# The output bias of a routed expert layer, taken off TensorE: ScalarE multiplies it by the gate, GpSimd adds it to the token rows

## The reference, cut to what matters

```python
logits = n @ Wr + br
probs = softmax(logits)
G, idx = max(probs), argmax(probs)        # gate and expert of the token
h1 = relu(n @ W1[idx] + b1[idx])
out = x + G * (h1 @ W2[idx] + b2[idx])    # b2 is the output bias
```

## Time and profile before

| what | value |
| --- | --- |
| time of 3 runs | median 529.25 us, 528.96 to 532.93 |
| the profiled execution | 533.77 us, of which the span is 532.0 us |
| mean granted TensorE clock | 0.986 of full speed |
| busy in the span | PE 486.3 us, DVE 429.0, ACT 335.7, POOL 81.9 |

### The profile page before, as it was taken

One profiled execution on the slowest core, in us unless ns is written; L12 is line 12 of the kernel. 1 busy time (PEld: TensorE's weight loads), 2 busy tenths in 40 slices (PEclk: granted clock), 3 DMA queues, 4 the chain that ended last, 5 costly groups with the idle time before them and its releaser, 6 DMA issues.

```text
span 532.0 us, 11423 instructions
## 1 busy us (share of the span) xinstructions
PE 486.3 (91%) x4369; PEld 361.9 (68%) x4370; DVE 429.0 (81%) x874; ACT 335.7 (63%) x636; POOL 81.9 (15%) x94
## 2 busy tenths in 40 slices
PE   3999999993899999999998999989899999999994
PEld 3877776761899998997887644444466697776662
DVE  7958889896999999876888778975877787986961
ACT  7356666668799999972775723435444558866820
POOL 5000000000000000001221201213244411222232
PEclk9999999997899999999999899999999999999999
DMA  7970000002011111001000293000011129975111
GB/s 200 311 275 1 1 2 1 2 1 103 2 51 55 56 72 71 2 10 72 2 1 1 99 329 146 1 0 4 1 42 42 62 66 380 338 236 182 55 57 55
DMA packets 25267, 45.10 MB, mean 85 GB/s; under 512 B 6977, under 2 KB 7013, under 8 KB 25212
## 3 DMA queue, kind: packets, MB, share of 16 engines
q1 hardware_dynamic: 23228, 39.16, 21.5%
q0 software_dynamic: 1952, 5.18, 2.6%
q10 hardware_dynamic: 32, 0.01, 0.0%
HBM read 33.23 MB, written 11.95 MB: 85 GB/s over the span
## 4 chain that ended last, share of the span: by engine, by line
PE 36%; DVE 20%; DMA 5%; issue 5%; POOL 4%; ACT 3%; POOLq 0%; DVEq 0%
PE sums L1690 13%; PE sums L1526 7%; PE sums L1703 5%; PE sums L1915 4%; DMA out<-aux 2%; DMA aux<-xperm_scratch 2%; DVE st L901 2%; POOL row L528 2%; PE sums L1886 2%; DVE work L1156 1%; PE sums L1504 1%; DVE big L1319 1%; POOL out L512 1%; PE sums L1680 1%; ACT rings L570 1%
## 5 line engine op out<-in xcount | busy, mean ns | idle before, releaser
L1690 PE MATMUL sums<-big,work 128*128 128x130 f16 x1080 | 66.4, 223 | 8.7 <-DVE work L1156 8.7
L1690 PEld LDWEIGHTS sums<-big,work 128*128 128x128 f16 x1080 | 63.7, 100 | 10.2 <-issue 6.2
L1591 PE MATMUL sums<-big 128*128 128x180 f16 x320 | 60.2, 272 | 1.0 <-DVE big L1005 1.0
L1005 DVE TENSOR_TENSOR big<-mid 128x1024 f16<-128x1024 f16 (+1 forms) x88 | 59.4, 732 | 0.0
L1791 PE MATMUL sums<-mid 128*128 128x512 f16 x200 | 47.2, 379 | 0.0
L1703 PE MATMUL sums<-big,mid 128*128 128x260 f16 x400 | 47.0, 275 | 0.1
L1550 PE MATMUL sums<-big,rings 128*128 128x512 f16 x120 | 45.2, 377 | 0.4
L595 ACT ACTIVATE mid<-sums 128x180 f32 x80 | 26.5, 332 | 28.6 <-PE sums L1598 27.7
L1703 PEld LDWEIGHTS sums<-big,mid 128*128 128x128 f16 x400 | 38.2, 96 | 7.5 <-issue 0.3
L683 ACT ACTIVATE aux<-aux,small 128x1250 f16<-128x1250 f32 x32 | 40.9, 1326 | 2.5 <-DVE work L1156 1.7
L683 ACT ACTIVATE mid<-aux,small 128x1250 f16<-128x1250 f32 x32 | 40.8, 1323 | 2.4 <-DVE work L1156 2.4
(11 more groups left out here) (322 smaller groups left out, 1098.8 us busy)
## 6 DMA issues: line engine op xcount, KB each, us to landing
big<-in_L_ffn_W SPq DMA_DIRECT2D x10, 1024.0 KB, 9.7
mid<-in_L_ffn_W SPq DMA_DIRECT2D x6, 1024.0 KB, 14.1
xperm_scratch<-work SPq DMA_DIRECT2D x1, 5753.0 KB, 18.7
aux<-thr_scratch SPq DMA_DIRECT2D x8, 640.0 KB, 3.8
aux<-xperm_scratch SPq DMA_DIRECT2D x8, 523.0 KB, 3.9
row<-in_x SPq DMA_DIRECT2D x1, 1280.0 KB
aux<-in_L_gnn_Ws SPq DMA_DIRECT2D x4, 256.0 KB, 4.6
row<-in_x SPq DMA_DIRECT2D x1, 1024.0 KB, 7.9
```

Source lines behind the costliest of these rows:

```text
L1005: return V.tensor_tensor(out.rearrange("p c (v two) -> p c v two", two=2), values.rearrange("p (v two) -> p v two", two=2).unsqueeze(1).to ...
L1591: mm(count_bank(base, k)[:, 0:RW], L_ring[:, slot, k * CH + j, :], R_ring[:, slot, k * CH + j, :], start=j == 0, stop=False)
L1690: ins = mm(acc_region(h, t), weighted[i // 2 % NC][:, s % 2, t * P:(t + 1) * P], VP[:, s, part, h, :, :].rearrange("p b f -> p (b f)"), st ...
```

## The change

b2 is no longer split, nor multiplied on TensorE; the 16 products, the selection matrix and the f16 parts go. SyncE loads the row of expert e, copied to all 128 partitions, into one of two buffers (`gb_bc`, `be_bc`), experts 0 and 1 ahead of the tokens, expert e (from 2) after `b2_scaled` has told that e - 2 is used up, and ahead of the load of the tokens of e + 2. VectorE makes the gate in a step of its own, `gate_of(e)`. ScalarE's `scale_bias(e)` multiplies the bias by the gate of each slot into `num_words`, a single buffer for both halves, so each half waits for GpSimd to have added the one before. GpSimd's `add_bias(e)` adds it to the rows in `xs`, once ScalarE has normalised them (`xs_normed`), and VectorE's `result(e)` waits for it (`b2_added`).

```diff
--- before.py
+++ after.py
@@ -211,8 +211,7 @@
         xT16, o = carve(work, 0, [2, 2, K, S1], F16)
         hT16, o = carve(work, o, [2, 2, K, S1], F16)
         h32 = xT_ring[:, :, :, :].rearrange("p a k m -> p (a k m)")[:, 0:4 * S1].rearrange("p (a b m) -> p a b m", a=2, b=2)
-        b2_nat = gb_bc[0:64, :]
-        b2_16 = be_bc[0:64, 0:D // 2].bitcast(F16)
+        b2_bc = [gb_bc, be_bc]
         W0T = [carve(work, 0, [2, D])[0][:, 0, :], carve(work, 0, [2, D])[0][:, 1, :], xh_ring[:, 0, :], xh_ring[:, 1, :]]
         thrT, _ = carve(rings, 0, [NP])
         hs, o = carve(work, 0, [2, D])
@@ -291,7 +290,6 @@
         iotaJ = sb("iotaJ", [P, NO])
         wr_sum = sb("wr_sum", [P, E1])
         valid = sb("valid", [P, 1])
-        pick16 = sb("pick16", [64, E1], F16)
 
         sums = ctx.enter_context(nc.psum_tensor("sums", [P, 8, 512], F32))
         bank = [sums[:, i, :] for i in range(8)]
@@ -402,9 +400,12 @@
             for e in range(3):
                 load_weights(e)
 
-            sp.wait_ge(sem("b2_zeroed"), 1)
-            for q in (0, 32):
-                sp.dma_start(b2_nat[q:q + E1, :], b2_d).then_inc(sem("ld_b2"), 16)
+            def load_bias(e):
+                sp.dma_start(b2_bc[e % 2][:, :], b2_d[e, :].partition_broadcast(P)).then_inc(sem(f"ld_b2_{e % 2}"), 16)
+
+            sp.wait_ge(sem("h_used"), T)
+            load_bias(0)
+            load_bias(1)
 
             sp.wait_ge(sem("scattered"), 16 * T)
             sp.wait_ge(sem("xs_psum"), 2)
@@ -422,6 +423,8 @@
                     sp.wait_ge(sem("w_lo0"), e - 2)
                     sp.wait_ge(sem("w_lo1"), e - 2)
                     load_weights(e + RW32 - 3)
+                sp.wait_ge(sem("b2_scaled"), 2 * (e - 1))
+                load_bias(e)
                 if e + 2 in range(RX, E1):
                     sp.wait_ge(sem(f"put{(e + 2) % RX}"), 32 * ((e + 2) // RX))
                     load_tokens(e + 2)
@@ -502,7 +505,6 @@
 
             g.wait_ge(sem("h_used"), T)
             nc.gpsimd.iota(slots, [[1, S1]], base=0, **kw)
-            nc.gpsimd.memset(b2_nat, 0.0).then_inc(sem("b2_zeroed"), 1)
 
             def put(e):
 
@@ -528,8 +530,21 @@
                     nc.gpsimd.tensor_tensor(x[:, t, :], x[:, t, :], rtmp[:, t % 2, :], ALU.add).then_inc(sem("x4_made"), 1)
                 if t >= 3:
                     scatter(t - 3)
+            def add_bias(e):
+
+                r = e % RX
+                if e:
+                    g.wait_ge(sem("xs_normed"), 2 * e)
+                for j, m in enumerate((P, S1 - P)):
+                    g.wait_ge(sem("b2_scaled"), 2 * e + j + 1)
+                    xr = xs[0:m, r, j, 0:D]
+                    nc.gpsimd.tensor_tensor(xr, xr, num_words[0:m, 0:D], ALU.add).then_inc(sem("b2_added"), 1)
+
+            add_bias(0)
             for e in range(E1):
                 put(e)
+                if e + 1 < E1:
+                    add_bias(e + 1)
             n = g.value_load(nspill[0:1, 0:1], min_val=0, max_val=NO)
             with g.If(n > 0):
                 g.wait_ge(sem("o_pos"), 1)
@@ -766,8 +781,6 @@
             w_hi(0, 0)
             w_hi(0, 1)
             a.wait_ge(sem("ff_used"), T)
-            a.wait_ge(sem("ld_b2"), 32)
-            act(b2_16, b2_nat, ACT.Copy, scale=WS).then_inc(sem("b2_hi"), 1)
 
             def relu(t):
                 a.wait_ge(sem("agg_done"), t + 1)
@@ -820,6 +833,16 @@
                     lg_x = xs[:, r, j, D + 3:ROW]
                     act(lg_x, lg_x, ACT.Exp, accum_out=gsum[:, r, j:j + 1]).then_inc(sem("gates_summed"), 1)
 
+            def scale_bias(e):
+
+                r = e % RX
+                a.wait_ge(sem(f"ld_b2_{e % 2}"), 16 * (e // 2 + 1))
+                a.wait_ge(sem("gate_made"), e + 1)
+                for j, m in enumerate((P, S1 - P)):
+                    if 2 * e + j:
+                        a.wait_ge(sem("b2_added"), 2 * e + j)
+                    act(num_words[0:m, 0:D], b2_bc[e % 2][0:m, :], ACT.Copy, scale=gate[0:m, r, j:j + 1]).then_inc(sem("b2_scaled"), 1)
+
             def x_hi(e):
 
                 if e >= 2:
@@ -850,12 +873,15 @@
             a.wait_ge(sem("ld_xs0"), 16)
             gates(0)
             w_hi(1, 1)
+            scale_bias(0)
             x_hi(2)
             for e in range(E1):
                 if e >= 1 and e + 2 < E1:
                     x_hi(e + 2)
                 if e + 1 < E1:
                     hidden(e + 1)
+                if e:
+                    scale_bias(e)
                 if e == 0:
                     rows(3)
                     w_hi(3, 0)
@@ -1321,9 +1347,6 @@
 
             split_w(0, 0)
             split_w(0, 1)
-            V.tensor_tensor(pick16[:, :], ident16[0:64, 0:E1], ident16[0:64, 32:32 + E1], ALU.add)
-            v.wait_ge(sem("b2_hi"), 1)
-            V.scalar_tensor_tensor(b2_16[32:64, :], b2_nat[32:64, :], WS, b2_16[32:64, :], ALU.mult, ALU.subtract).then_inc(sem("b2_lo"), 1)
 
             def logits(t):
 
@@ -1428,26 +1451,35 @@
                     link(V.tensor_copy(hT16[:, e % 2, 0, f, :], h32[:, q, :, :]))
                     V.tensor_tensor(hT16[:, e % 2, 1, f, :], h32[:, q, :, :], hT16[:, e % 2, 0, f, :], ALU.subtract).then_inc(sem("h_lo16"), 1)
 
+            def gate_of(e):
+
+                r = e % RX
+                v.wait_ge(sem("gates_summed"), 2 * (e + 1))
+                V.reciprocal(gate[:, r, :], gsum[:, r, :]).then_inc(sem("gate_made"), 1)
+                v.wait_ge(sem("gate_made"), e + 1)
+                link(V.tensor_scalar(gate_ws[:, r, :], gate[:, r, :], 1.0 / WS, None, ALU.mult))
+
             def result(e):
 
                 r = e % RX
                 at_least(v, "xs_normed", 2 * e)
                 names(e)
-                v.wait_ge(sem("gates_summed"), 2 * (e + 1))
-                link(V.tensor_scalar(gate[:, r, :], gsum[:, r, :], WS, None, ALU.mult))
-                link(V.reciprocal(gate_ws[:, r, :], gate[:, r, :]))
                 for j, m in enumerate((P, S1 - P)):
                     v.wait_ge(sem("m2_done"), 2 * e + j + 1)
+                    v.wait_ge(sem("b2_added"), 2 * e + j + 1)
                     V.scalar_tensor_tensor(xs[0:m, r, j, 0:D], bank[4 + 2 * (e % 2) + j][0:m, :], gate_ws[0:m, r, j:j + 1],
                                            xs[0:m, r, j, 0:D], ALU.mult, ALU.add).then_inc(sem("res_made"), 1)
 
             h_split(0)
             x_lo(1)
             split_w(2, 0)
+            gate_of(0)
             result(0)
             x_lo(2)
             split_w(1, 1)
             for e in range(E1):
+                if e >= 1:
+                    gate_of(e)
                 if e >= 1 and e + 2 < E1:
                     x_lo(e + 2)
                 if e + 1 < E1:
@@ -1908,16 +1940,14 @@
                     pe.wait_ge(sem("res_made"), 2 * (e - 1))
                 for j in blocks:
                     m = (P, S1 - P)[j]
-                    mm(bank[4 + 2 * (e % 2) + j][0:m, :], pick16[:, e:e + 1].to_broadcast([64, m]), b2_16, start=True, stop=False)
                     for n, (k, (wp, hp_)) in enumerate((k, c) for k in range(K) for c in PARTS):
                         if n % (K // 2 * len(PARTS)) == 0:
                             pe.wait_ge(sem("h_lo16"), 2 * e + k // 2 + 1)
                         ins = mm(bank[4 + 2 * (e % 2) + j][0:m, :], hT16[:, e % 2, hp_, k, j * P:j * P + m],
-                                 W16[e % 2][1][:, wp, k, :], start=False, stop=n == 3 * K - 1)
+                                 W16[e % 2][1][:, wp, k, :], start=n == 0, stop=n == 3 * K - 1)
                     ins.then_inc(sem("m2_done"), 1)
 
             m1_first()
-            pe.wait_ge(sem("b2_lo"), 1)
             m2(0, (0,))
             pe.wait_ge(sem("te_ready"), 1)
             token_T(1)
```

## The result

The changed kernel took 542.16 us (median of 4 runs, 539.2 to 542.69), the kernel before 529.76 us beside it (4 runs, 528.96 to 532.93). The ratio is 1.0199, with a 95% interval of 1.0149 to 1.0249: the change makes it slower. By the ratio that is 10.5 us (7.9 to 13.2); the two medians lie 12.4 us apart. The forecast was 539 us, in a range of 532 to 545.

A forecast was written before the change was run, and what follows sets the result against it. TensorE was taken to bound the kernel, VectorE close behind. Layouts gave +10.4 or +9.1, taken as +10.0, less 0.5 before the loop: +9.5 on 533.77 us makes 543.3, or 539 us on the median, range 532 to 545.

The forecast's parts named there:

- Bias products: TensorE in the expert loop: removing 16 bias products wins 5.3 us, a turn becoming 10.4 us if nobody needs more.
- Prices: New steps in the loop: ScalarE scale 0.75 us, GpSimd add 1.10 us (upper end 2.07), hand-over some 0.05 us.
- Before the loop: First tile's statistics no longer wait for VectorE's selection matrix and low part: -0.5 us taken, between 0 and -0.7.
- The first result: Scale and add steps ahead of the loop's first result start m1(2) 2.6 us late; m1(3), m1(4) recover to +1.9, +1.7.
- The circle of 10.7 us a turn: Loop: gate, scale, add, scale, w_hi, split, token numbers and result, split sum to 10.7 us, already as long as TensorE's 10.4.
- Tokens without reserve: Loop: late put of expert 2 delays token load and everything behind rows(6); m1(6) starts at 504.5 instead of 497.7, +6.8 us.
- TensorE waiting for x_lo in three turns or more: Sign expected in the changed kernel's loop profile: TensorE waits for VectorE's x_lo in at least three turns.
- The end: From expert 6's second result to the kernel's end, expert 7's adds standing behind put(6): 9.8 us, where it was 9.1.
- The sum: Whole kernel: +10.0 us from the layouts, -0.5 before the loop, so +9.5 on 533.77, giving 543.3 us.
- Without that exclusion the layout ends 6 us earlier: Loop and end: if GpSimd adds and VectorE's two-input instructions did not block each other, the laid-out kernel ends 6 us earlier.
- no exclusion: Rival: adds touch VectorE in few places, so only first result, circle and end count: +3.4 to +5.1, 533 us; chance 0.14.
- long-adds rival: Rival: adds meet splits each turn (1.5 us mean) or TensorE's clock falls in new waits: +13 to +16, 544 us; chance 0.16.

The follow-up runs named there:

- e1: The changed kernel with the bias left out altogether (no scale, no add, no waits for them; gate step stays): 528.44 us, ratio 0.993 to the kernel before.
- e11: The kernel before, bias products kept, with selection matrix and f16 bias parts made just ahead of the expert loop: 531.81 us, ratio 0.9968.
- e12: The changed kernel with only the next expert's gate made earlier, right behind the hidden split: 540.93 us, ratio 1.0159 to the kernel before.
- e5: The changed kernel run again, unaltered, in the second group of runs: 541.49 us, ratio 1.0175 to the kernel before.
- e2: The changed kernel with each GpSimd add replaced by two fills that read no SBUF, waits kept, bias left out: 538.83 us, ratio 1.0124 to before.
- e9: The changed kernel with fills for adds, second scale buffer, early gate and last adds first; bias left out: 531.86 us, ratio 0.9961 to before.
- e3: The changed kernel with a second scale buffer, early gate, and expert 7's adds ahead of put(6): 536.94 us, ratio 1.007 to the kernel before.
- e4: The changed kernel with idle TensorE products ahead of m1(2) and of expert 5's transposes: 540.39 us, ratio 1.0159 to the kernel before.
- e6: The kernel before, bias products kept, plus two GpSimd adds on spare words behind each put, waited for by nobody: 538.06 us, ratio 1.0099.

## Why the prediction was right, by its steps

- **Bias products, -5.3 us.** Gone, and a turn of 10.20 us exists. But as a gift to the whole it was too large: e1 has 3.7 us, products and start together, and TensorE waits 3.7 us for token rows there, 1.3 before.
- **Prices.** Scale taken at 0.75, measured 0.72. Add taken at 1.10, measured 1.09 alone and 1.19 and 1.32 on the mean, beside VectorE.
- **Before the loop, -0.5.** Measured 0.70 in the trace of after and 0.74 in e11.
- **The first result, +2.6.** 2.58 of wait; m1(2) 2.4 us later, counted from the loop's start. But m1(3) and m1(4) did not catch up to +1.9 and +1.7, they stood at +3.0 and +2.9: the turn behind the wait ran at a granted clock of 0.86, 6.01 us for an m1 of 4.44, which I had not laid out.
- **The circle of 10.7 us a turn.** Three turns of 10.2 to 11.0, 10.6 on the mean, agree roughly; that one is shorter than the circle shows that it does not bind every turn. Of its members, GpSimd's add was waited for 16.2 us. VectorE's reciprocal was named once, 2.2 us, and the 4.3 us put down to "issue" are it too: in all five cases the scale starts 0.08 or 0.09 after the reciprocal's end, as at 521.41. e12 shows that an earlier gate buys nothing clear.
- **Tokens without reserve.** The mechanism held and the place was one expert off: expert 5, behind the put of expert 1 at 472.25, not expert 6 behind that of expert 2. That m1(6) then starts at 69.4 for 69.3 is luck to that extent: the long turn came one turn early, behind a start that was 1.2 us later than laid out.
- **TensorE waiting for x_lo in three turns or more.** Wrong. It waited for x_lo once; the other waits were at the transposes, for ScalarE's token rows. I had followed the late tokens through w_hi, split and x_lo, but TensorE meets them first at the transposes.
- **The end, 9.8 us from the second result of expert 6.** 10.1 us. The last subtraction waited for an add, so m2(7) did as well, and the result waited 3.77 and 1.33 us.
- **The sum.** +9.5 on the profiled execution, as forecast: +10.2 from the loop's start on and -0.7 before it. The execution came out 1.2 us under the 543.3 because 1.06 us of it were won in untouched code. The traces account for 9.5 us; the ratio of the first runs gives 10.5 (7.9 to 13.2), their medians 12.4, and those of e5 9.4. With a start of the loop that moves by up to 5 us from one execution to the next, the times can't tell these apart.

What held only by cancelling is the split of the loss. "Without that exclusion the layout ends 6 us earlier" is the term mis-sized. In the traces, taking the reading adds away saves 2.6 us with the chain as it is (e2) and 3.2 with the chain eased (e9 against e3), about half of the 6. The rest of the layout's +10.4 (its ends, 538.2 and 527.9, give 10.3), that is the chain less what TensorE gives back, was then to be 4.4; it is 7.6, which is what e2 still has over before. 4.4 + 6 and 7.6 + 2.6 come to nearly the same sum, and so the forecast came out right.

The times point the same way with wide intervals: 2.7 us from e5 to e2 in ratio, not clear of nothing, and 5.8 from e3 to e9. By the traces the two parts nearly add up, 2.6 and 6.6 for 9.8 together. The rival "no exclusion" at 533 was too cheap: e2 is that case, 7.6 us over before in the loop less the 0.7 ahead of it, against the 3.4 to 5.1 given; its time alone (6.3 us, 4.0 to 9.2) does not decide that. What the prediction had left out of the exclusion is the cast, which with its one input was lengthened too (e3). Of the long-adds rival, both halves happened a little, longer adds and a fallen clock. It said that the clock would cost little, since TensorE would not be the bound there; e4 shows 2.7 us in the trace, more than nothing. That it costs so much because m1(2) and the transposes of expert 5 stand on the way to the next results is argued, not shown.

In the rows the granted clock is 0.50 right behind the waits of 2.58 and 4.03 us, and 1.00 before them. By the Trainium skill (TensorE: Matmul & The Clock Gate, Part 1) a TensorE that idles goes down to 1.2 GHz, half speed; the two stretches agree.

Left open: how much each single wait of the chain is worth. Three parts removed together bring 6.6 us in the trace; one by one 4.0 (two buffers), 1.0 at the end (last adds first; its other 1.1 can't be its doing) and -0.8 (gate early). They are single executions, and the times resolve none of the three. That an early gate pays only with the second buffer is argued, from e12, where the wait moves to the next semaphore.

## What to carry to other kernels

An engine's idle share does not make it a free place for work: GpSimd stood idle for at least half of each turn, and 20 us of adds there, with their scales, cost 13 us, while 12 us on VectorE, busy for 10.96 of 11.10 in the early turns, cost 2.6. Before moving a step to another engine, count the hand-overs that it puts between two things already waited for, and lay the turn out through all of them. Easing one of several waits in a circle can show nothing, as the early gate did, so remove them together too before calling them innocent. Where executions differ by as much as the effect in code that they share, count from the first instruction of the stretch that was changed. Where TensorE is made shorter, ask what lands next: here the waits for tokens took about a third of the gift.

## What the hardware showed that I had not expected

- A cast of VectorE with one SBUF input is kept out by a reading add too: 2.86 us instead of 0.38 (e3). I had counted only the subtractions. Fills hold it up as well, to 427 ns on the mean in e2 and 551 in e9, where it has 384 before.
- The result, of whose two large inputs one comes from PSUM, keeps its 0.75 us although it starts inside an add (e3: 450.05, the add from 449.89 to 450.99).
- A weight split can be held up too: at 483.13 in e6 it takes 3.55 us instead of 2.28, with GpSimd on a put until 483.22 and on two adds right behind.
- Two adds back to back were one block in e3: the waiting VectorE instruction did not get in between them. In the same kernel an instruction of two columns took 2.86 us at 521.75, where it takes 0.16.
- A put lengthens from 0.92 or 1.00 to 2.28 us where it meets a weight split (472.25 and 519.85), and up to 3.56 (452.16); the splits keep their 2.28. The kernel before has this too: its 16 puts take 22.2 us, 24.7 with the change, so it is a small part of the loss.
- 16 adds that nobody waits for cost 1.0% (e6): 2.5 us in the loop and 2.2 because the last two run behind the last put.
